# The first two expert lists' one-hot placing reads its numbers from PSUM

## The reference

```python
k = int(EXPERT_CAPACITY * t / e)             # 2 * 2048 / 8 = 512
scores = jnp.einsum('ntd,ed->nte', x, gate_w)
probs = jax.nn.softmax(scores, axis=-1)
g, m = jax.lax.top_k(probs.transpose(0, 2, 1), k)
xin = x[batch_idx, m]
h = jnp.einsum('nekd,edf->nekf', xin, w1)
h = jax.nn.gelu(h, approximate=False)
h = jnp.einsum('nekf,efd->nekd', h, w2)
out = jnp.zeros((n, t, d), dtype=x.dtype).at[batch_idx, m].add(g[..., None] * h)
```

## Time and profile before

| what | value |
|---|---|
| three runs | 1862.68, 1865.25, 1865.76 us; median 1865.25 |
| profiled execution, its own time | 1863.54 us |
| its span, first to last instruction | 1861.7 us |
| TensorE busy | 1721.4 us, 92% |
| VectorE busy | 1477.8 us, 79% |
| ScalarE busy | 1378.8 us, 74% |
| GpSimd busy | 1371.4 us, 74% |
| chain that ended last | TensorE 76%, GpSimd 7%, VectorE 6%, ScalarE 4%, issue 6% |
| granted TensorE clock, mean | 0.977 |

### The profile page before, as it was taken

The page is one execution under the profiler, slowest core; times in us unless marked ns, Lnnn a source line. Parts: engine busy times, 40 slices in busy tenths (PEclk is TensorE's granted clock), DMA queues, the critical chain, the costliest instruction groups (busy, mean ns, idle before and its releaser), DMA issues.

```text
span 1861.7 us, 34289 instructions
## 1 busy us (share of the span) xinstructions
PE 1721.4 (92%) x12348; PEld 1484.2 (80%) x12348; DVE 1477.8 (79%) x3114; ACT 1378.8 (74%) x2705; POOL 1371.4 (74%) x644
## 2 busy tenths in 40 slices
PE   6688999999999999999999999998875999999998
PEld 5567788887878888787888878787665888899997
DVE  3557888888888888888888888888898688766664
ACT  3468878888887888888788888877642766566664
POOL 0009899898989989898998989899999334444443
PEclk9999999999999999999999999999897999999999
DMA  4012222222132222313322231323122434555552
GB/s 195 1 40 64 62 66 69 67 61 86 50 86 67 69 65 62 87 49 87 67 68 66 62 87 49 87 61 79 61 60 85 139 95 119 136 137 133 136 134 29
DMA packets 120888, 149.88 MB, mean 81 GB/s; under 512 B 8208, under 2 KB 111120, under 8 KB 120336
## 3 DMA queue, kind: packets, MB, share of 16 engines
q1 hardware_dynamic: 108432, 130.91, 25.1%
q0 software_dynamic: 12288, 16.79, 5.2%
HBM read 121.98 MB, written 17.30 MB: 75 GB/s over the span
## 4 chain that ended last, share of the span: by engine, by line
PE 76%; POOL 7%; issue 6%; DVE 6%; ACT 4%; DMA 0%; POOLq 0%; DVEq 0%; ACTq 0%
PE po L1819 9%; PE pD L1119 9%; PE pY L1136 9%; PE ph L1819 9%; PE pA L718 6%; POOL room L1177 3%; PE pA L620 3%; PE pB L915 3%; PE pB L925 3%; POOL room L1187 3%; DVE room L1168 3%; PE pB L1215 3%; PE pB L946 2%; PE pA L646 2%; PE pA L611 2%
## 5 line engine op out<-in xcount | busy, mean ns | idle before, releaser
L1187 POOL TENSOR_TENSOR room<-room 128x1024 f32<-128x1024 f32 x256 | 605.8, 2367 | 179.7 <-DVE room L1102 141.2
L1168 DVE TENSOR_TENSOR_SCAN room<-pD,last,room 128x256 f32<-128x256 f32 x1024 | 691.7, 731 | 50.2 <-PE pD L1119 38.7
L1177 POOL TENSOR_TENSOR room<-room 128x1024 f32<-128x1024 f32 x256 | 605.7, 2366 | 64.1 <-PE pY L1136 63.2
L1149 ACT ACTIVATE room<-room,fixed,kkT 128x512 f32<-128x512 f32 x512 | 406.4, 806 | 54.6 <-PE pD L1119 52.6
L1119 PE MATMUL pD<-fixed,room 128*128 128x128 f32 x2048 | 318.4, 279 | 47.2 <-DVE room L1168 45.1
L1136 PE MATMUL pY<-fixed,room 128*128 128x128 f32 x2048 | 319.1, 280 | 15.8 <-POOL room L1177 15.8
L1119 PEld LDWEIGHTS pD<-fixed,room 128*128 128x128 f32 x2048 | 243.6, 144 | 75.2 <-issue 41.3
L1136 PEld LDWEIGHTS pY<-fixed,room 128*128 128x128 f32 x2048 | 249.3, 145 | 65.7 <-POOL room L1177 29.3
L330 POOL DMA_INDIRECT xg<-xn_rows,W x64 | 69.3, 1082 | 198.1 <-DVE W L324 183.0
L1778 ACT ACTIVATE h<-ph 128x512 f32<-128x512 f32 x128 | 76.6, 598 | 135.6 <-PE ph L1819 108.1
L1819 PE MATMUL po<-w_up,h_up 128*128 128x256 f32 x512 | 149.1, 291 | 3.2 <-DVE h_rest L1686 2.6
(11 more groups left out here) (310 smaller groups left out, 3584.4 us busy)
## 6 DMA issues: line engine op xcount, KB each, us to landing
room<-kq_rows SPq DMA_DIRECT2D x256, 256.0 KB, 5.2
w_in<-w_d SPq DMA_DIRECT2D x32, 1024.0 KB
room<-ndS SPq DMA_DIRECT2D x16, 512.0 KB, 3.3
xt<-x_in SPq DMA_DIRECT2D x16, 256.0 KB, 3.0
y_out<-xo SPq DMA_DIRECT2D x16, 256.0 KB, 2.1
xn_rows<-xnC SPq DMA_DIRECT2D x16, 256.0 KB, 2.1
W<-weights SPq DMA_DIRECT2D x1, 1808.0 KB, 9.1
W<-weights SPq DMA_DIRECT2D x1, 1697.5 KB, 16.6
```

The lines of the kernel that those rows point to most:

```text
L1149: act.activation(decT[:, m % 2, t, :], turn2(ndT, it, NT * DI, t * DI, DI), ACT.Identity, bias=ones_s[:, 0:1], scale=turn2(kkT, it, NT * D ...
L1168: dve.tensor_tensor_scan(run, pD[h][:, k2 * TB:(k2 + 1) * TB], run, last[:, bass.ds(later(it) * (DS * DT) + m * DT + k, 1)], ALU.mult, ALU ...
L1177: pool.tensor_tensor(sq[:, m % 2], st[:, m % 4], kqb[:, m % SLOTS, 1, :].unsqueeze(1).broadcast_to([P, DT, TB]), ALU.mult).then_inc(sem("r ...
L1187: pool.tensor_tensor(st[:, m % 4], turn2(u, it, DT * TB).rearrange("p (k t) -> p k t", k=DT), kqb[:, m % SLOTS, 0, :].unsqueeze(1).broadca ...
```

## The change

For batch 0 the last step of the choice also writes the low numbers of lists 0 and 1 (the first 32 columns) into columns 0 to 31 of the bank, and their quarters (32 x 4) into the columns `b`, which are free by then. The two calls of `place` in the last turn read these in place of the copies in SBUF. The SBUF copies are still written, and lists 2 to 15 still read them. All other instructions and their order are the same.

```diff
+NEAR = 2 * TT
...
             do(dve.tensor_copy(self.lo[:, at], loi))
+            if b == 0:
+                do(dve.tensor_copy(self.near(bank)[0], loi[:, 0:NEAR]))
             do(dve.tensor_scalar(loi, posi, 7, None, ALU.arith_shift_right))
             do(dve.tensor_copy(hi, loi))
+            if b == 0:
+                do(dve.tensor_tensor(self.near(bank)[1], hi[:, 0:NEAR].unsqueeze(2).broadcast_to([P, NEAR, SL]),
+                                     self.iota[:, 0:SL].unsqueeze(1).broadcast_to([P, NEAR, SL]), ALU.is_equal))
             do(dve.tensor_tensor(self.quarter[:, at, :], hi.unsqueeze(2).broadcast_to([P, LB, SL]),
                                  self.iota[:, 0:SL].unsqueeze(1).broadcast_to([P, LB, SL]), ALU.is_equal))
 
-    def place(self, dve, k):
+    def near(self, bank):
+        a, w = BANK_AT["b"]
+        return bank[:, 0:NEAR], bank[:, a:a + w].rearrange("p (n c) -> p n c", c=SL)
+
+    def place(self, dve, k, bank=None):
...
         at = slice(k * TT, (k + 1) * TT)
+        lo, quarter = (self.lo, self.quarter) if bank is None else self.near(bank)
         dve.tensor_tensor(
             self.entries[:, k % 2],
             self.value[:, :, at].rearrange("p a t -> p t a").unsqueeze(3).broadcast_to([P, TT, PARTS, SL]),
-            self.quarter[:, at, :].unsqueeze(2).broadcast_to([P, TT, PARTS, SL]), ALU.mult)
+            quarter[:, at, :].unsqueeze(2).broadcast_to([P, TT, PARTS, SL]), ALU.mult)
         dve.tensor_tensor(self.onehot[:, k % 2], self.iota.unsqueeze(1).broadcast_to([P, TT, P]),
-                          self.lo[:, at].unsqueeze(2).broadcast_to([P, TT, P]), ALU.is_equal)\
+                          lo[:, at].unsqueeze(2).broadcast_to([P, TT, P]), ALU.is_equal)\
...
-                    select.place(dve, k)
+                    select.place(dve, k, pA[0])
```

## The result

| | median | runs | ratio to before (95%) |
|---|---|---|---|
| before | 1865.25 us | 9, 1862.68 to 1868.05 | |
| changed | 1859.95 us | 9, 1857.94 to 1861.02 | 0.997 (0.9962 to 0.9979) |
| changed, once more, beside other kernels | 1859.12 us | 7, 1856.48 to 1860.78 | 0.9971 (0.996 to 0.9983) |

The change makes the kernel 5.3 us faster by the medians; by the interval it is 3.9 to 7.1 us. I predicted 1860.95, 4.3 us faster, and gave 0.58 to a gain of over 0.2%.

What follows compares the result with a forecast made beforehand. List 0's entries product, held on VectorE by GpSimd's product, was taken to bound the path: 4.06 us saved, 4.45 with the DMA wait gone, less 0.15 for the clock, gives 4.3; 1865.25 becomes 1860.95, range 1858.0 to 1864.2.

Steps and rivals of the forecast that it cites:

- (a): Choice's last step: the two new instructions take 0.56 us, fit into VectorE's 0.69 us of idle time, cost nothing.
- (b): List 0's entries product with its quarters in PSUM: 0.40 us in place of 4.46, saving 4.06 us.
- (d): TensorE behind list 0's placing: the whole chain shifts by 4.06 us, leaving TensorE free for the rows' turning at 1444.39.
- (f): TensorE's clock after a shorter idle gap: gain between 0.95 and 6.6 us; a loss of 0.15 booked, leaving 4.3.
- (e): List 0's gathers: first takes 0.96 us, not 2.73; rows land before TensorE is free; turning starts 4.45 us earlier.
- The other signs: Entries product under 0.6 us, first gather near 1, GpSimd's three products without gap; wrong if clock 0.50 through projection.
- (g): Behind 1454 nothing is fixed in time, so the whole 4.3 us gain reaches the kernel's end.
- the clock stays up: Rival: TensorE's clock stays high after the shorter gap, gain 6.6 us, time 1858.7; 8%.
- Not one of SBUF inputs: Rival: the hold of list 0's entries product isn't one of SBUF inputs, no change, 1865.3 us; 7%.
- slower: Rival: TensorE meets the first expert's matmuls with the clock still at 0.50, 1866.8 us; 5%.
- late clock: Rival: the clock comes back late in the projection or behind it, gain 1 to 2.5 us, about 1863.3; 17%.

Runs made afterwards that it cites:

- one-hots only: Changed kernel, but the entries product reads its quarters from SBUF again and only the one-hot products read PSUM: 1861.5 us, ratio 0.9981 to the kernel before.
- writes only: Changed kernel's two new instructions in the choice's last step, but both placings read SBUF as before: 1864.02 us, ratio 0.9996 to the kernel before.
- entries only: Changed kernel, but the one-hots of lists 0 and 1 read SBUF again and only the entries product reads PSUM: 1863.68 us, ratio 0.9995 to the kernel before.

## Why the prediction was right, and where it wasn't

(a) The two new instructions at no cost: right, none that can be told (0.9996 alone, 0.9987 to 1.0005).

(b) The hold of list 0's entries product, 4.06 us: right. The one-hots were ready 3.99 us sooner from P. No PSUM extra was seen (0.47 against 0.48 us). That two SBUF inputs are the cause is shown: the entries product took 0.46 and 0.47 us beside GpSimd's products with one input in PSUM and 4.06 to 4.59 with both in SBUF (before, one-hots only, writes only), the hold went to the next such instruction when the first was freed, and a product of four columns with both in SBUF was held for 7.19 us. The Trainium skill's rule ("SBUF — State Buffer", section "SBUF: two separate sides") agrees on who holds whom, for GpSimd's products in both directions. My reading of it, that the two take turns, doesn't hold here: the four-column product stood waiting while three GpSimd products that began after it went ahead.

(d) and (f) All shifts by 4.06, and what the clock adds and takes about cancels: right in the sum, but neither part had a size of its own in it. The clock stayed up from the small matmuls to 1441.9, P + 11.8 (0.65 over 1441 to 1444), where before it had fallen near 1437.1, P + 8.1 (0.89 over 1434 to 1438); the sums took 1.51 us and not 2.80, and the turning was 5.73 us early and not 4.45, 1.28 more. Behind it the clock took 1.29 back. I had named both ends (1.2 us more before the turning, up to 3.5 less behind) and taken the middle, a loss of 0.15. 4.44 us in the stretch against 4.3 is thus partly luck. With extra matmuls that keep the clock up behind the sums, 1.6 us come back in one profile.

(e) The rows at P + 13.9 to 14.5: right (14.1). "Of the gathers' 1.77 us nothing more is gained": this failed. It is also one of the signs by which I had said I'd be wrong: the turning still waits for the gathered rows. With TensorE 5.7 us early it waits 0.95 us for them; with list 1's placing left in SBUF the kernel loses 1.9 us by the medians, and with only the one-hots changed it gains 1.9 to 5.2 over the kernel before where I expected 0.4. I treated the clock's course as fixed and so TensorE's chain as the later one. The two chains lay within 0.4 us in the profile before, and which is last changes with the clock. The other signs came out as forecast, but for the clock, which was at 0.50 for the turning and through most, not all, of the projection. And I didn't look at what the splits let go: had the gathers stayed held, the weight load would have come before the rows.

(g) All of it reaches the end: the profiles don't contradict it, within what they vary among themselves. From the first expert's first matmul to the end it was 407.8 us before, 408.6 and 407.0 in two profiles of the changed kernel. The medians' 5.3 us is more than the 4.4 of one pair of profiles. Three profiles with VectorE's hold and the long gather in place (before, entries only, writes only) have 24.97, 25.43 and 26.56 us from P to the first expert, two of the changed kernel 20.53 and 20.41: means 25.65 and 20.47, a difference of 5.2. That fits, from few samples. The clock has a share in it that wasn't separated. The mean granted clock of each run is on record: 0.976 on average for the kernel before, 0.978 to 0.979 for the changed one. At the same mean of 0.979, five runs with the two new instructions alone lay at 1862.5 us on average and six of the changed kernel at 1859.0. As an estimate from these, some 3.5 of the 5.3 us are there at a like clock, and the rest goes with the clock.

Of the rivals, "the clock stays up" was half true: it stayed up to 1441.9. "Not one of SBUF inputs" and "slower" fell. The late clock came, at 1.29 us of its 3.5.

## What to carry to other kernels

When an instruction is held with no semaphore to explain it, compare its end with the end of GpSimd's work, and count its SBUF inputs; one input moved into free PSUM columns freed it here. Every instruction of a group that runs beside GpSimd's work has to be moved: the next one with two SBUF inputs takes over the wait. When two chains end within a few tenths, shortening either can be worth more than the wait seen in one profile, and making the other faster alone can cost, if it lets a large transfer go in front of a small one that is awaited.

## What the runs showed of the hardware beyond what I expected

- A held VectorE instruction doesn't get in between GpSimd products that follow one another at once: four columns waited 7.19 us, over the end of one product and three whole ones, and came through when GpSimd had a gap.
- GpSimd's side is held too: a product of 2.36 us took 4.05 beside a 2.28 us VectorE product with two SBUF inputs, and gathers of 0.96 us took 2.72 to 3.07 beside the 2048-column product with two SBUF inputs, 1.14 and 1.15 beside it with one in PSUM. Beside weight splits some took 1.32 and 1.49 and others 0.95 to 1.11; what decides isn't shown.
- Rows of a list came 2.7 to 2.9 us behind the start of its fourth gather with no load in front of them, and 4.4 to 4.6 us behind it with a 1 MB load in front.
- A float32 matmul of 128 x 128 stands in the trace as two instructions, together some 0.23 us at full clock (24 of them in 5.52 us).
